# Four-layer graph network on one core: 12 of the last layer's 49 dense row steps moved from the attention projection into the second mean aggregation

## The chip, the cores and the metric

The kernel runs on one core of a Trainium2 chip. The metric is the device time of one execution in microseconds (us), lower is better. The engines are named as in the profile: PE (matrix engine), DVE (vector engine), ACT (scalar engine), POOL (GpSimd, which issues the indirect transfers) and SP (the queue that issues the plain transfers).

## The reference

There are 50,000 nodes with 128 features and 25,000 edges, whose destinations are sorted. Four layers follow each other, each a residual with a layer norm:

```python
x = _layernorm(x + _L0_gnn_ref(x, edge_attr_64, W, b, src, dst))       # gated messages, summed by destination
x = _layernorm(x + _L1_gnn_ref(x, edge_index_t, kernel, attention))    # attention, scores clipped to -2..2
x = _layernorm(x + _L2_gnn_ref(x, edge_index, 0, W1l, b1, W1r, W2l, b2, W2r))
x = _layernorm(x + _L3_gnn_ref(x, edge_index, qw, kw, ln_gamma, ln_beta, out_w, out_b))

def _L2_gnn_ref(...):                    # two mean aggregations
    h = relu(_sage(x, src, dst, W1l, b1, W1r))
    return _sage(h, src, dst, W2l, b2, W2r)
def _sage(x, src, dst, Wl, b, Wr):
    return _mean_aggr(x, src, dst, n) @ Wl.T + b + x @ Wr.T

def _gat_forward(x, ...):                # layer L3
    Q, K = x @ qw, x @ kw                # per head, 4 heads of 32
    alpha = (Q[:, row] * K[:, col]).sum(-1) / scale
    a = exp(alpha - seg_max[col]); a = a / denom[col]
    h = segment_sum(Q[:, row] * a, col)
    h = layernorm(h) * ln_gamma + ln_beta
    return (h * sigmoid(h)) @ out_w + out_b
```

A node without an incoming edge has `h = 0` in the last layer, so its result is `layernorm(x + c)` with one constant row `c`. The kernel computes that for all 50,000 nodes first (the "dense rows") and then overwrites the rows of the nodes that have edges.

## The kernel before, in words

Edge rows lie in 128 partitions of 196 slots. A step handles J = 4 slots of each partition, so a stage over the edges has 49 steps (`STEPS`); one step of the dense rows handles 8 rows of each partition, 1024 nodes, and there are 49 of these as well (`DENSE_STEPS`; the last, the tail, has 848 nodes).

The program is a list of stages, each with its own loop on every engine. The function `pipeline(eng, looped, stages, per)` writes such a loop: a list of (lag, function, count), where in iteration s the function handles step s - lag. The first and last iterations are written out, the others run in a hardware loop of `per` iterations a turn. The order within an iteration is the order of the list, and each engine executes its instructions strictly in that order. Engines wait for each other through semaphores only (`wait_done`: the step is finished; `wait_free`: the buffer's last use two steps ago is finished; `wait_landed`, `wait_drained`: a transfer in or out of the buffer has completed).

The stages that matter here:

- **gat**, the attention of layer L1 (about 545 to 1015 us). DVE adds up each step's scores in `add_others`, `add_scores`, `leaky_scores` and `clip_scores`. Each used a semaphore of its own (`others`, `e0`, `e1`, `e2`).
- **sage2**, the second mean aggregation (about 1914 to 2180 us). In a step POOL gathers 4 times 128 source rows (L803; buffers four steps deep), DVE sums them by destination (L1634, `running_sum`), takes the means (L2080, L2084), PE transposes and multiplies (L961, L1161 to L1169), ACT copies the transposes out (L1277, `sage_copies`), DVE takes the moments of the sum (`x3_moments`, L2133, L1587, lag 2), ACT the square root (L1254, lag 2), DVE inverts it (`x3_shifts`, L1612, L1602, L1598, lag 3), and ACT writes the normed rows (`new_x3`, L1427, lag 3). SP loads two row blocks and stores two for each step. The loop is four iterations a turn.
- **att1**, the attention projection (about 2182 to 2500 us). In a step POOL gathers again, DVE passes node rows back along the runs (L1877, `spread_row`, four a step), PE transposes both and multiplies by the query and key weights (L1192, L1198), ACT copies out (L1277 twice, L1449, L1452), DVE multiplies and sums per head (L2161, L2165, lag 2). All 49 dense steps ran here, one an iteration: SP loads 512 KB (L607), DVE adds the constant row (`nodes_x3_more`, L2172), takes the moments (L1581, L1587, `nodes_x3_moments`), ACT takes the root (L1254, lag 1), DVE inverts and makes the shifts (L2184, L1598, lag 1), ACT writes 8 normed rows a partition (L1268, lag 1) and SP stores 512 KB (L614, lag 2). The loop is two iterations a turn.

The dense steps wrote into rings of two buffers, `node_in` and `node_out`; `own_rows` was a ring of two too.

## Time and profile before

| | us |
|---|---|
| median of 3 runs (lowest to highest) | 2859.24 (2841.92 to 2860.3) |
| time of the profiled execution | 2861.17 |
| span of the profiled execution | 2859.5 |
| DVE busy in it | 2280.2 (80%) |
| PE, ACT, POOL busy | 1851.7, 1735.6, 1698.8 |

The span is what the profile draws. The time of an execution is what the runs measure, here 1.7 us more than its span. An engine's busy share over the whole span says little in this program, because every stage is limited by something else. It is read stage by stage.

### The profile page before, as it was taken

What the parts mean: (1) busy time and instruction counts of PE and PEld (TensorE: products, weight loads), DVE (VectorE), ACT (ScalarE), POOL (GpSimd) and SP (SyncE); (2) the same over time, 40 slices, a digit from 0 to 9 for tenths busy, and PEclk for the clock granted to TensorE, in tenths of its full rate; (3) what the DMA queues carried; (4) which work ended last, traced back from release to release, by engine and by line L of the source; (5) the groups of instructions that cost most, each with busy time, mean ns of one, the idle gap of its engine ahead of it and who ended that gap; (6) DMA issues with size and microseconds to landing.
All of it is one profiled execution on the core that took longest, in us unless ns stands there. A gap on an engine that the chain in (4) does not pass through costs nothing. (4 is left out here: it accounts for less than half of the span.)

```text
span 2859.5 us, 51576 instructions
## 1 busy us (share of the span) xinstructions
PE 1851.7 (65%) x9787; PEld 1368.6 (48%) x9787; DVE 2280.2 (80%) x9061; ACT 1735.6 (61%) x4459; POOL 1698.8 (59%) x1605
## 2 busy tenths in 40 slices
PE   5676766466666626777777666658886666656673
PEld 4565656344544414445455333336665555534442
DVE  7887887899999927887788688857776999888882
ACT  3554545333333316887778688864555888858885
POOL 7777777266656664333333666637776776327775
PEclk8777777789888867998899899989997888767876
DMA  6777877445444437999899788868886888734441
GB/s 202 240 245 230 256 247 236 139 79 85 79 79 84 71 52 256 350 330 325 325 338 344 248 291 291 298 216 252 265 263 211 292 295 294 264 136 160 163 160 52
DMA packets 280133, 625.06 MB, mean 219 GB/s; under 512 B 51230, under 2 KB 84649, under 8 KB 280055
## 3 DMA queue, kind: packets, MB, share of 16 engines
q1 hardware_dynamic: 207543, 523.73, 53.6%
q0 software_dynamic: 72512, 100.52, 16.1%
q14 instruction: 58, 0.48, 0.1%
q8 instruction: 20, 0.33, 0.0%
HBM read 342.76 MB, written 285.23 MB: 220 GB/s over the span
## 5 line engine op out<-in xcount | busy, mean ns | idle before, releaser
L1268 ACT ACTIVATE node_out<-node_in,n_shift,n_root 128x128 f32<-128x128 f32 (+1 forms) x1176 | 468.1, 482 | 85.5 <-DVE n_shift L1598 85.4
L795 POOL DMA_INDIRECT sums<-gat_sums,dst_safe_i x196 | 185.7, 948 | 306.1 <-DVE pre L2027 256.5
L916 POOL DMA_INDIRECT out_dram<-node_x2t,out_index x196 | 208.7, 1065 | 156.7 <-ACT node_x2t L1485 96.3
L803 POOL DMA_INDIRECT src_rows<-x_table,row_i x200 | 201.4, 1007 | 129.9 <-issue 52.2
L803 POOL DMA_INDIRECT sums<-x_table,row_i x192 | 193.8, 1010 | 87.3 <-issue 50.0
L1581 DVE BATCH_NORM_STATS2 n_stats<-node_in 128x6 f32<-128x256 f32 (+1 forms) x588 | 209.4, 419 | 25.4 <-DMA node_in<-y_nodes 14.2
L862 POOL DMA_INDIRECT gat_sums<-src_rows,add_idx x100 | 160.9, 1609 | 112.9 <-issue 24.7
L803 POOL DMA_INDIRECT own_rows<-in_x_dram,dst_safe_i x196 | 191.1, 975 | 59.7 <-issue 58.8
L1277 ACT ACTIVATE t_a<-ps 128x512 f32<-128x512 f32 (+1 forms) x198 | 115.8, 585 | 175.0 <-PE ps L961 167.9
L862 POOL DMA_INDIRECT gat_sums<-sums,add_idx x96 | 153.5, 1599 | 92.9 <-issue 31.7
L961 PE MATMUL ps<-ident,msg 128*128 128x128 f32 x590 | 105.3, 305 | 122.5 <-DVE msg L2111 57.4
L1277 ACT ACTIVATE t_b<-ps 128x512 f32<-128x512 f32 (+1 forms) x198 | 115.9, 586 | 104.7 <-PE ps L961 104.6
L961 PE MATMUL ps<-ident,own_rows 128*128 128x128 f32 x588 | 101.9, 302 | 94.2 <-DMA own_rows<-in_x_dram,dst_safe_i 90.0
L961 PEld LDWEIGHTS ps<-ident,msg 128*128 128x128 f32 x590 | 72.3, 154 | 179.4 <-issue 131.4
L1090 PE MATMUL ps<-node_x2t,w1r_t 128*128 128x512 f32 x196 | 110.1, 689 | 56.2 <-ACT node_x2t L1368 55.6
L1192 PE MATMUL ps<-qw_sb,t_a 128*128 128x128 f32 x392 | 71.9, 340 | 96.1 <-ACT t_a L1277 96.1
L1101 PE MATMUL ps<-w2r_t,node_h1t 128*128 128x128 f32 (+1 forms) x784 | 126.8, 311 | 0.0
L961 PEld LDWEIGHTS ps<-ident,own_rows 128*128 128x128 f32 x588 | 75.5, 154 | 101.7 <-DMA own_rows<-in_x_dram,dst_safe_i 97.2
L1039 PE MATMUL ps<-alpha,node_in 128*128 128x196 f32 x392 | 95.2, 397 | 40.6 <-DVE junk L1917 38.2
L837 POOL DMA_INDIRECT src_rows<-in_x_dram,src_i x100 | 100.3, 1003 | 30.4 <-issue 30.2
L1634 DVE SCALAR_TENSOR_TENSOR acc<-acc,keep,src_rows 128x129 f32<-128x129 f32 x200 | 71.1, 356 | 58.9 <-DMA src_rows<-h_table,row_i 32.8
L1101 PEld LDWEIGHTS ps<-w2r_t,node_h1t 128*128 128x128 f32 (+1 forms) x784 | 106.2, 210 | 22.7 <-issue 22.7
(424 smaller groups left out, 6618.9 us busy)
## 6 DMA issues: line engine op xcount, KB each, us to landing
own_rows<-x_table SPq DMA_DIRECT2D x245, 256.0 KB, 3.3
node_in<-in_x_dram SPq DMA_DIRECT2D x96, 512.0 KB
x_table<-node_out SPq DMA_DIRECT2D x96, 512.0 KB
x_table<-new_rows SPq DMA_DIRECT2D x147, 256.0 KB
gat_sums<-node_x2t SPq DMA_DIRECT2D x49, 528.0 KB, 4.0
acc_dump<-acc SPq DMA_DIRECT2D x98, 264.0 KB
node_sums<-gat_sums SPq DMA_DIRECT2D x48, 528.0 KB
h_table<-node_h SPq DMA_DIRECT2D x48, 512.0 KB, 5.2
```

The lines of the kernel that those rows point to most:

```text
L795: g_.indirect_dma_start(out=to[:, g.b, j, 0:width], out_offset=None, in_=tab, in_offset=bass.IndirectOffsetOnAxis(ap=indices(j), axis=0)). ...
L803: g_.indirect_dma_start(out=to4[g.q][:, j, 0:F], out_offset=None, in_=tab, in_offset=bass.IndirectOffsetOnAxis(ap=indices(j), axis=0)).the ...
L837: g_.indirect_dma_start(out=src4[g.q][:, j, 0:F], out_offset=None, in_=x[:, :], in_offset=bass.IndirectOffsetOnAxis(ap=at_tile(src_i, g, j ...
L862: g_.indirect_dma_start(out=gat_sums[:, :], out_offset=bass.IndirectOffsetOnAxis(ap=add_idx[:, g.q, j:j + 1], axis=0), in_=src4[g.q][:, j, ...
L916: g_.indirect_dma_start(out=out[:, :], out_offset=bass.IndirectOffsetOnAxis(ap=out_index[:, t:t + 1], axis=0), in_=wide_new[:, g.b, j, :], ...
L961: last = te.transpose(ps[bank][g.b][:, j * F:(j + 1) * F], tiles[:, j, 0:F], ident[:, :])
L1039: last = te.matmul(ps[0][j // 2][:, at], past_at[g.b][:, j * P:(j + 1) * P], slot_score[:, :], start=True, stop=True)
L1090: last = te.matmul(ps[1][h][:, :], w1r_t[:, :], node_x2t[:, g.b, h * J * F:(h + 1) * J * F], start=True, stop=True)
L1101: last = te.matmul(ps[3][bank][0:pn, i * F:(i + 1) * F], node_h1t[:, g.b, j * F:j * F + pn], w2r_t[:, :], start=False, stop=i == J - 1)
L1268: last = sc.activation(to[0:pn, g.b, j, :], rows[0:pn, g.b, j, 0:F], ACT.Identity, bias=NORM[k][2][0:pn, g.b, j:j + 1], scale=root[0:pn, j ...
L1277: sc.activation(to[:, g.b, 0:jn * F], ps[bank][g.b][:, 0:jn * F], ACT.Copy).then_inc(L[copied].sem, 1)
L1581: last = v.bn_stats(NORM[k][0][0:pn, g.b, j:j + 2, :].rearrange("p j c -> p (j c)"), rows[0:pn, g.b, j:j + 2, 0:F].rearrange("p j f -> p f ...
```

## The change

Of the 49 dense steps of the last layer, 12 (`SPACED`) are moved into sage2, one in every fourth iteration; the remaining 37 stay in att1, in three of every four iterations (36 and the tail). `spaced(lag, stage)` calls a stage for those steps s whose s mod 4 is 0, `packed(lag, stage)` for those whose s mod 4 is 0, 1 or 2. On SP the spaced loads have a lag of 1 and the stores a lag of 5; on DVE the moments have a lag of 2 and the inverses 3; on ACT the root has 2, the first four of the eight rows 3 and the last four 4. The spaced steps use one buffer, the packed steps three (a third input and a third output buffer come from `node_y`). In att1 the loops of SP, ACT and DVE become four iterations a turn, `own_rows` becomes four buffers deep (`own4`), and SP's loads and stores get other lags. SP now waits for the end of the dense stores of layer L2 before sage2 instead of before att1. In gat the semaphores `others`, `e0` and `e1` become one, `scored`, which counts three a step. No arithmetic is changed.

```diff
+SPACED = 12
+def wait_third_free(eng, signal, g):
+    if isinstance(g, Spaced):
+        eng.wait_ge(signal.sem, g.index() + signal.base)
+    elif isinstance(g.of4, int) and g.of4 == 0:
+        eng.wait_ge(signal.sem, signal.base + SPACED)
+    else:
+        eng.wait_ge(signal.sem, g.index() + (signal.base - 2))
+def spaced(lag, stage):
+    def turn(g):
+        if g.q == 0 and not (isinstance(g.of4, int) and g.of4 >= SPACED):
+            stage(Spaced(g))
+    return (lag, turn, STEPS)
+def packed(lag, stage):
+    def turn(g):
+        if g.q < 3:
+            stage(Packed(g))
+    return (lag, turn, STEPS)
...
-        PER = {"accd": J, "ended": J, "spread": J, "dpe": 2, "dact": 2}
+        PER = {"scored": 3, "accd": J, "ended": J, "spread": J, "dpe": 2, "dact": 2}
...
+            def load_last_nodes(g):
+                D = flow["nodes4"]
+                wait_third_free(sp, D["n_row"], g)
+                for lo, hi in parts(g):
+                    sp.dma_start(in3[g.b][lo:hi, :, :], node_rows(x3_table, SLOTS, g)[lo:hi]).then_inc(rows_in3.sems[g.b], 16)
...
             L = flow["sage2"]
             wait_all(sp, flow["sage1"]["stored"])
+            wait_all(sp, flow["nodes3"]["n_out"])
...
-            pipeline(sp, STEPS, edges((0, both), (1, dump), (4, store)))
+            pipeline(sp, STEPS, edges((0, both), (1, dump), (4, store)) + [spaced(1, load_last_nodes), spaced(5, store_last_nodes)], per=4)
...
-            pipeline(sp, DENSE_FULL, edges((0, load_own_back(L, x3_table, own_rows))) + [nodes(0, load_nodes(D, x3_table, SLOTS, "n_row"))]
-                     + edges((2, store_q)) + [nodes(2, store_nodes(D, out, 0))])
+            pipeline(sp, DENSE_FULL, edges((0, load_own4)) + [packed(1, load_last_nodes)]
+                     + edges((3, store_q)) + [packed(3, store_last_nodes)], per=4)
...
-            pipeline(act, STEPS, edges((3, new_x3), (2, root), (0, sage_copies)), per=4)
+            pipeline(act, STEPS, edges((3, new_x3), (2, root)) + [spaced(2, last_node_root)] + edges((0, sage_copies))
+                     + [spaced(3, last_node_rows(0, J)), spaced(4, last_node_rows(J, DJ))], per=4)
...
-            pipeline(act, DENSE_FULL, [nodes(1, roots(D, "n")), nodes(1, normed_rows(D, "n", node_in, node_out, "n_row", "n_out"))]
-                     + edges((1, queries_keys_out), (0, att_copies)))
+            pipeline(act, DENSE_FULL, [packed(1, last_node_root), packed(1, last_node_rows(0, DJ))]
+                     + edges((1, queries_keys_out), (0, att_copies)), per=4)
...
-            pipeline(dve, STEPS, edges((3, x3_shifts), (0, sources_landed), run[0], run[1], (2, x3_moments), run[2], run[3],
-                                       (0, means)), per=4)
+            pipeline(dve, STEPS, edges((3, x3_shifts), (0, sources_landed), run[0], run[1], (2, x3_moments), run[2], run[3], (0, means))
+                     + [spaced(3, last_inverses), spaced(3, last_shifts), spaced(2, last_more), spaced(2, last_moments)], per=4)
...
-            pipeline(dve, DENSE_FULL, edges(spread[0]) + [nodes(1, node_inverses)] + edges(spread[1]) + [nodes(1, node_shifts)]
-                     + edges(spread[2], (2, products), spread[3], (2, score_sums)) + [nodes(0, nodes_x3_more), nodes(0, nodes_x3_moments)])
+            pipeline(dve, DENSE_FULL, edges(spread[0]) + [packed(1, last_inverses)] + edges(spread[1]) + [packed(1, last_shifts)]
+                     + edges(spread[2], (2, products), spread[3], (2, score_sums)) + [packed(0, last_more), packed(0, last_moments)], per=4)
```

DVE in sage2, the end of one iteration and the start of the next, before (`acc`, `msg` and `edge` are the sums, means and counts; `e_root`, `e_shift` the norm of the edge rows):

```order
L2080 RECIPROCAL edge<-acc 128x4 [waits accd]
L2084 TENSOR_SCALAR msg<-acc,edge 128x128 [waits rcp,tr_a]
L2084 TENSOR_SCALAR msg<-acc,edge 128x128 x3
L1612 RECIPROCAL e_root<-e_root 128x4 [waits e_rt]
L1602 TENSOR_TENSOR e_root<-e_root,canon 128x4 [waits e_rc]
L1598 SCALAR_TENSOR_TENSOR e_shift<-e_stats,e_root 128x4 [waits scaled]
```

The same place after, in an iteration that carries the moments of a dense step (one of four):

```order
L2200 RECIPROCAL edge<-acc 128x4 [waits accd]
L2204 TENSOR_SCALAR msg<-acc,edge 128x128 [waits rcp,tr_a]
L2204 TENSOR_SCALAR msg<-acc,edge 128x128 x3
L2262 TENSOR_TENSOR node_in<-node_in,local_bc 128x1024 [waits n_in0]
L2270 BN_STATS n_stats<-node_in 128x6 [waits n_row,n_pre]
L2270 BN_STATS n_stats<-node_in 128x6 x3
L2274 TENSOR_SCALAR n_root<-n_stats 128x8 [waits n_bn]
L1732 RECIPROCAL e_root<-e_root 128x4 [waits e_rt]
L1722 TENSOR_TENSOR e_root<-e_root,canon 128x4 [waits e_rc]
L1718 SCALAR_TENSOR_TENSOR e_shift<-e_stats,e_root 128x4 [waits scaled]
```

Six dense instructions now stand between the means of one step and the norm of an earlier step.

ACT in sage2 after, in the iteration that carries the dense root (`node_out` rows follow later):

```order
L1545 ACTIVATE new_rows<-ps,e_shift,e_root 128x128 [waits e_nm,stored1]
L1545 ACTIVATE new_rows<-ps,e_shift,e_root 128x128 x3
L1352 ACTIVATE e_root<-e_root 128x4 [waits e_ve]
L1375 ACTIVATE n_root<-n_root 128x8 [waits n_ve]
L1395 ACTIVATE t_a<-ps 128x512 [waits mm,tr_a]
L1395 ACTIVATE t_b<-ps 128x512 [waits mm,tr_b]
```

Before, the copies `t_a` and `t_b` stood right behind the root of `e_root`. Now the dense root, which waits for DVE's dense moments, stands ahead of them.

DVE in att1 before, one iteration (they were all alike):

```order
L1877 SCALAR_TENSOR_TENSOR msg<-msg,undone,own_rows 128x128 [waits spread,tr_b,own1]
L2184 RECIPROCAL n_root<-n_root 128x8 [waits n_rt]
L1877 SCALAR_TENSOR_TENSOR msg<-msg,undone,own_rows 128x128 [waits spread]
L1598 SCALAR_TENSOR_TENSOR n_shift<-n_stats,n_root 128x8 [waits n_rc]
L1877 SCALAR_TENSOR_TENSOR msg<-msg,undone,own_rows 128x128 [waits spread]
L2161 TENSOR_TENSOR pre<-new_rows,gate 128x512 [waits score,cp_c,newd]
L1877 SCALAR_TENSOR_TENSOR msg<-msg,undone,own_rows 128x128 [waits spread]
L2165 TENSOR_REDUCE alpha<-pre 128x16 [waits pre]
L2172 TENSOR_TENSOR node_in<-node_in,local_bc 128x1024 [waits n_in1]
L1581 BN_STATS n_stats<-node_in 128x6 [waits n_nm,n_row,n_pre]
```

The same engine after: the fourth iteration, which has no dense moments (and ends at the TENSOR_REDUCE), and the next one, which has no inverse and no shift:

```order
L2314 TENSOR_REDUCE alpha<-pre 128x16 [waits pre]
L1997 SCALAR_TENSOR_TENSOR msg<-msg,undone,own_rows 128x128 [waits spread,tr_b,own0]
L1997 SCALAR_TENSOR_TENSOR msg<-msg,undone,own_rows 128x128 [waits spread] x2
L2310 TENSOR_TENSOR pre<-new_rows,gate 128x512 [waits score,cp_c,newd]
L1997 SCALAR_TENSOR_TENSOR msg<-msg,undone,own_rows 128x128 [waits spread]
L2314 TENSOR_REDUCE alpha<-pre 128x16 [waits pre]
L2262 TENSOR_TENSOR node_in<-node_in,local_bc 128x1024 [waits n_in0]
```

So in four iterations three dense steps are left on DVE, with their instructions in the order they had.

## Rows read from the trace of the kernel before

**Rows 1.** Busy time by stretch: gat, sage2, att1; PE, PEld, DVE, ACT, POOL, clock, DMA, GB/s

```profile
600.00:1000.00 400.00, 261.42 (x1430) 193.91 (x1431) 372.56 (x2022) 127.41 (x339) 252.09 (x159) 0.89 0.49 81
1942.00:2142.00 200.00, 166.76 (x1064) 125.13 (x1063) 149.42 (x599) 101.47 (x274) 151.53 (x160) 1.00 0.82 260
2200.00:2450.00 250.00, 159.56 (x953) 143.69 (x952) 225.46 (x555) 210.96 (x520) 176.94 (x169) 0.81 0.88 295
```

**Rows 2.** Groups of instructions in sage2 (1942 to 2142): count, busy, mean, idle before

```profile
L803 POOL DMA_INDIRECT sums<-h_table,row_i x80 | 76.4, 955 | 24.4 <-issue 20.7 <-DVE acc L1634 3.7
...
L1634 DVE SCALAR_TENSOR_TENSOR acc<-acc,keep,sums 128x129 f32<-128x129 f32 x80 | 28.5, 356 | 20.3 <-DMA sums<-h_table,row_i 13.1 <-issue 1.3
```

**Rows 3.** Timeline of DVE in sage2, two iterations: start, duration, idle before

```profile
2011.21 0.23 DVE L1612 RECIPROCAL e_root<-e_root 128x4 f32<-128x4 f32 x1
...
2012.26 0.85 DVE L1634 SCALAR_TENSOR_TENSOR acc<-acc,keep,sums 128x129 f32<-128x129 f32 x2 [0.28 <-issue]
...
2015.12 0.88 DVE L2084 TENSOR_SCALAR msg<-acc,edge 128x128 f32<-128x128 f32 x4
2015.91 0.17 DVE L1612 RECIPROCAL e_root<-e_root 128x4 f32<-128x4 f32 x1
...
2017.30 0.86 DVE L1634 SCALAR_TENSOR_TENSOR acc<-acc,keep,sums 128x129 f32<-128x129 f32 x2 [0.73 <-DMA sums<-h_table,row_i]
...
2020.96 0.17 DVE L1612 RECIPROCAL e_root<-e_root 128x4 f32<-128x4 f32 x1
```

**Rows 4.** Timeline of ACT in sage2, one iteration

```profile
2016.90 0.60 ACT L1277 ACTIVATE t_a<-ps 128x512 f32<-128x512 f32 x1 [1.99 <-issue]
...
2017.87 1.51 ACT L1427 ACTIVATE new_rows<-ps,e_shift,e_root 128x128 f32<-128x128 f32 x4
2019.24 0.23 ACT L1254 ACTIVATE e_root<-e_root 128x4 f32<-128x4 f32 x1
```

**Rows 5.** Timeline of DVE in att1, two iterations

```profile
2299.87 0.35 DVE L1877 SCALAR_TENSOR_TENSOR msg<-msg,undone,own_rows 128x128 f32<-128x128 f32 x1 [0.59 <-issue]
...
2302.70 1.22 DVE L2172 TENSOR_TENSOR node_in<-node_in,local_bc 128x1024 f32<-128x1024 f32 x1
...
2305.56 0.42 DVE L1587 TENSOR_SCALAR n_root<-n_stats 128x8 f32<-128x8 f32 x1
2306.00 0.35 DVE L1877 SCALAR_TENSOR_TENSOR msg<-msg,undone,own_rows 128x128 f32<-128x128 f32 x1
...
2306.76 0.16 DVE L1598 SCALAR_TENSOR_TENSOR n_shift<-n_stats,n_root 128x8 f32<-128x8 f32 x1
...
2312.44 0.35 DVE L1877 SCALAR_TENSOR_TENSOR msg<-msg,undone,own_rows 128x128 f32<-128x128 f32 x1 [0.59 <-issue]
```

**Rows 6.** Timeline of ACT in att1, one iteration

```profile
2306.01 0.21 ACT L1254 ACTIVATE n_root<-n_root 128x8 f32<-128x8 f32 x1
2306.96 3.19 ACT L1268 ACTIVATE node_out<-node_in,n_shift,n_root 128x128 f32<-128x128 f32 x8 [0.74 <-DVE n_shift L1598]
2310.05 0.58 ACT L1449 ACTIVATE new_rows<-ps 128x512 f32<-128x512 f32 x1
...
2311.96 0.21 ACT L1254 ACTIVATE n_root<-n_root 128x8 f32<-128x8 f32 x1
```

**Rows 7.** Timeline of PE in att1, in the same iteration

```profile
2305.66 1.91 PE L1192 MATMUL ps<-qw_sb,t_a 128*128 128x128 f32 x8 [2.78 <-ACT t_a L1277]
...
2309.62 0.60 PE L961 MATMUL ps<-ident,msg 128*128 128x128 f32 x4
```

**Rows 8.** Groups of instructions in att1 (2182 to 2500)

```profile
L803 POOL DMA_INDIRECT src_rows<-x_table,row_i x99 | 104.9, 1059 | 41.9 <-issue 28.2 <-PE ps L961 13.7
...
L2172 DVE TENSOR_TENSOR node_in<-node_in,local_bc 128x1024 f32<-128x1024 f32 (+1 forms) x49 | 59.6, 1217 | 1.1 <-DMA node_in<-x_table 1.0
```

**Rows 9.** Timeline of POOL in att1, the gather that overlaps a dense addition of DVE

```profile
2303.03 1.70 POOL L803 DMA_INDIRECT sums<-x_table,row_i  x1 [0.30 <-issue]
2305.04 0.94 POOL L803 DMA_INDIRECT sums<-x_table,row_i  x1 [0.30 <-issue]
```

**Rows 10.** Timeline of DVE in gat, around the second addition of the scores

```profile
802.35 0.16 DVE L1974 TENSOR_TENSOR key<-key 128x4 f32<-128x4 f32 x1
802.47 0.16 DVE L1932 TENSOR_TENSOR edge<-edge 128x4 f32<-128x4 f32 x1
```

124 lines of the change are left out of this document (93 added, 31 removed).

## The prediction

> **What bounds the kernel now.** I read the busy time by stretch first, then the timelines of the two stages that the change touches, because the share of the whole span mixes them.
>
> In sage2 POOL is the pace. It issues 160 gathers in 200 us, 1.25 us each, so a step of four takes 5.0 us [rows 1]. Busy time says 151.5 of 200 only, but 0.30 us stands before each gather in which POOL waits for nothing that another engine could give [rows 2]. DVE waits for gathered rows instead: 13.1 us in this stretch for half of its steps [rows 2]. PE runs at a granted clock of 1.00, the DMA engines are 0.82 busy at 260 GB/s [rows 1].
>
> In att1 DVE is the pace. Two iterations take 12.57 us (2299.87 to 2312.44) [rows 5], 25.1 us for four, and DVE is 90% busy (225.5 of 250 us) [rows 1]; one of the two iterations begins with 0.59 us of "issue", the turn of the loop [rows 5]. ACT is close behind: from root to root 5.95 us (2306.01 to 2311.96), its only idle time 0.74 us, for DVE's shift [rows 6]. POOL needs 1.06 + 0.30 us a gather, 5.4 us a step [rows 8], and so has 0.8 us to spare.
>
> The work moves from a stage where DVE has little slack to one where it had none. The question is whether sage2's slack is large enough.
>
> **sage2: what a dense step costs there.** First the slack. The iteration from 2011.21 to 2015.91 had no wait for rows (0.28 us "issue" only) and took 4.70 us; the next took 5.05 with 0.73 us of waiting, 4.60 without what exceeds the 0.28 [rows 3]. So DVE alone needs 4.65 us a step, 18.6 us for four, and the gathers allow 20.0. Slack: 1.4 us in four steps.
>
> Then the load. From the dense addition to the variance is 2.86 us (2302.70 to 2305.56) and the variance takes about 0.17 more [rows 5] (0.42 in the row shown; I take the shorter, that of other small operations such as the one at 2306.76). Inverse and shift are two small operations, 0.2 and 0.16 us, with a drain between them: 0.45. Together 3.5 us. 18.6 + 3.5 = 22.1 us for four steps, and DVE is the pace.
>
> Then ACT. In the iteration with the dense moments the dense root stands ahead of the copies, and it waits until DVE has done the moments, 3.0 us after the means. That delays PE's product, but DVE's next moments are two iterations off, so it is covered. Further on it is not: ACT's copies of step 4i are through 1.9 us after the means (2016.00 to 2017.87) [rows 3, 4]; then come four dense rows, 1.55 us (half of 3.09, from 2306.96 to 2310.05) [rows 6]; then `new_x3`, 1.37, and the root, 0.23 [rows 4]. That is 5.05 us, and DVE asks for the root after 4.65. DVE waits some 0.4 us once in four steps, or nothing if the stage runs ahead there. I take 22.4 us for four, and 12 x (22.4 - 20.0) = **+29 us**. Bounds: if the 3.5 us shrinks by what small waits absorb, 21.5, +18; the high end comes with the rivals.
>
> What is hidden: ACT's dense work, 3.1 + 0.2 us in four steps on an engine that is busy 101 of 200 us [rows 1]. SP's loads and stores: SP now waits for the rows of the dense step before (one buffer), and behind that wait stand the loads of the own rows of the next step; these are needed more than one iteration later, so 2 us of delay have cover. Four iterations of slack in the gather buffers keep POOL going through DVE's 3 us. The earlier wait of SP for the layer L2 stores costs nothing that I can find: POOL's first gather of sage2 comes after sage1's last scattered row, long after the last dense store was issued.
>
> The lengthened gather: one that overlaps the dense addition took 1.70 us, not 0.94 [rows 9]. In sage2, where POOL is the pace, that would be 0.76 us a dense step, 20.8 us for four. It stays under DVE's 22.4, so it adds nothing. [...]
>
> **att1: what is saved.** DVE loses the 3.5 us of one dense step in four and one of two loop turns (0.6): 25.1 - 4.1 = 21.0 us. That is a floor, not the time. POOL: 16 x 1.36 = 21.8, less the lengthened gather of one addition, 21.4. And the ring through ACT: root, DVE's inverse, second spread and shift, eight rows, query, gate and two copies take 5.95 us [rows 6], three times in four iterations: 17.9. The fourth iteration has no rows; there ACT's copies wait for PE, which multiplies and transposes for 4.56 us (2305.66 to 2310.22) [rows 7] at a clock of 0.81 [rows 1], and then ACT copies again. From copy to copy this is 4.8 us as the row shows it and some 3.6 if PE ran at full clock; I take 4.4, nearer to the row. 17.9 + 4.4 = 22.3 us, and the ring is the pace. 12 x (22.3 - 25.1) = **-34 us**; bounds -44 (POOL's floor, 21.4) and -19 (23.5, if the short iteration delays the next one too). DVE hardly waited for its own rows, so the deeper ring of these gives nothing more. The wait of DVE's products for the gate of two steps ago, new in the short turn, is about 0.5 us and lies inside the 22.3.
>
> **gat: the merged semaphore.** `add_scores` started 0.12 us after the operation before it [rows 10]. It now waits for a register operation that computes three times the step number and stands behind another wait. DVE is 93% busy there [rows 1], so 0.1 us a step shows: 49 x 0.1 = 5 at most, **+4 us**, bounds 0 and 8. Nothing in the trace shows this operation in this place.
>
> **Sum.** -34 + 29 + 4 = -1 us on the profiled execution of 2861 us. The median of the runs is 2859.2, so 2858 us. What 12 dense steps give back in att1 they take in sage2, because DVE's slack there is 1.4 us in four steps and a dense step needs 3.5.
>
> **Rivals.**
>
> *A, sage2 is cheap and att1 gives all it can.* DVE's small waits overlap with the dense operations (21.5 us for four, +18), att1 reaches POOL's floor (-44), gat costs nothing: -26, **2833 us**. For it: the idle gaps of 0.1 to 0.3 us on DVE may be filled. Against: they are drains between dependent operations and stay.
>
> *B, POOL stays the pace in sage2.* The move costs the lengthened gathers only: 20.8 us for four, +9; with -34 and +4 this is -21, **2838 us**. [...] For it: POOL is the pace today. Against: DVE's 22.1 us, which nothing hides.
>
> *C, slower: sage2's transfers.* Four steps move 4 x 1288 KB (gathered 256, own 2 x 256, dumped 264, stored 256), 5.3 MB, which fits the 260 GB/s of the stage. A dense step adds 1024 KB: 6.3 MB. At 260 GB/s that takes 24.3 us, +52 in all; with -34 and +4 this is +22, **2881 us**, and with att1 at its weak end +37. It decides from 22.4 us for four steps on, which is 282 GB/s. The place where it would show is the gathered rows landing late although POOL is ahead. For it: the DMA engines are 0.82 busy and would be 0.97 by proportion at an unchanged 20 us. Against: 295 GB/s at 0.88 in att1 [rows 1], where dense transfers take part.
>
> *D, the short iteration in att1 disturbs its neighbours.* Three long iterations after a short one do not settle at 5.95; 23.5 us for four, -19: in all +14, **2873 us**.
>
> *E, it does not do what it says*: the moved steps leave att1 at POOL's pace. That is the floor of 21.4 us in A, and it limits no more than the ring does.
>
> **How the numbers follow.** My forecast has 0.48, A 0.15, B 0.10, C 0.15, D 0.12. A measurement of this kernel tells about 1% (29 us) from no change. The likeliest case has 2858, with its own bounds 2843 to 2870. The range 2834 to 2882 takes in B, D, most of A and half of C, and leaves out less than 2 in 10. Faster by over 1% (below 2831) needs A and more: 0.16. Slower by over 1% (above 2888) needs C with D: 0.17. Within 1%: 0.67.
>
> **What would show it.** In sage2, DVE's waits for gathered rows almost vanish and POOL's waits for DVE's sums grow; four steps take 22.4 us, and the stage grows by some 29 us. PE's clock may fall below 1.00. Gathers that overlap the dense addition take 1.7 us. In att1 four steps take about 22.3 us, with one short iteration, and ACT's wait for the shift is 0.7 us throughout. In gat a step grows by about 0.1 us. I am wrong if sage2 keeps 20 to 21 us for four steps, or if att1 shrinks by less than 20 us.

## Result and the profile after

The changed kernel takes 2861.59 us (median of 16 runs, 2848.62 to 2872.06), the kernel before 2849.52 us in the runs beside it (16 runs). The ratio is 1.0042, with a 95% interval of 1.0025 to 1.0059: 12 us slower, where -1 was forecast. A second comparison, in another session, gives 1.0021 (1.0004 to 1.0037), 6 us. The profiled execution takes 2862.23 us, 1 us more than the profiled one of before (2861.17 us), which is longer than all 16 runs of that kernel (highest 2860.3). So the two traces alone hide what the medians show, and a good part of the study is about that.

Busy time by stretch of the kernel after, with the columns of [rows 1] (the att1 stretch is 210 us long here, since the stage starts later):

```profile
600.00:1000.00 400.00, 273.65 (x1424) 203.16 (x1423) 371.07 (x2014) 125.56 (x334) 249.52 (x156) 0.84 0.48 79
1942.00:2142.00 200.00, 158.04 (x962) 117.11 (x960) 161.62 (x604) 120.24 (x330) 149.40 (x150) 0.97 0.86 285
2240.00:2450.00 210.00, 140.65 (x899) 127.95 (x898) 177.91 (x447) 166.68 (x398) 164.90 (x148) 0.85 0.84 280
```

In sage2 POOL issued 150 gathers in 200 us instead of 160, and DVE is busy 12 us longer. The granted clock is 0.97 instead of 1.00. The groups of the same stretch (compare [rows 2]):

```profile
L900 POOL DMA_INDIRECT sums<-h_table,row_i x77 | 75.0, 974 | 27.5 <-issue 21.0 <-DVE acc L1754 6.5
...
L1754 DVE SCALAR_TENSOR_TENSOR acc<-acc,keep,sums 128x129 f32<-128x129 f32 x72 | 25.6, 355 | 10.3 <-issue 1.5 <-DMA sums<-h_table,row_i 1.4 <-DMA acc_dump<-acc 1.2
```

DVE's 13.1 us of waiting for gathered rows are down to 1.4, and POOL waits 6.5 us for DVE in this group where it waited 3.7: the pace has passed to DVE, though POOL's buffers hide most of that within this stretch. POOL's gathers are also longer here, 974 ns on average instead of 955. The timeline of DVE in sage2 has the dense operations in one iteration and the wait for ACT's root three iterations later:

```profile
2044.44 1.21 DVE L2262 TENSOR_TENSOR node_in<-node_in,local_bc 128x1024 f32<-128x1024 f32 x1
2045.77 1.42 DVE L2270 BATCH_NORM_STATS2 n_stats<-node_in 128x6 f32<-128x256 f32 x4
...
2062.28 0.18 DVE L1732 RECIPROCAL e_root<-e_root 128x4 f32<-128x4 f32 x1 [0.32 <-ACT e_root L1352]
...
2066.87 1.20 DVE L2262 TENSOR_TENSOR node_in<-node_in,local_bc 128x1024 f32<-128x1024 f32 x1
```

From addition to addition, four steps, it is 22.43 us (2044.44 to 2066.87). At the end of the stage POOL, which had been up to four steps ahead, stands still until DVE has caught up and the last sums are dumped:

```profile
2172.79 0.95 POOL L900 DMA_INDIRECT src_rows<-h_table,row_i  x1 [0.30 <-issue]
...
2192.49 0.95 POOL L912 DMA_INDIRECT fix_acc<-acc_dump,fix_idx  x1 [16.26 <-DMA acc_dump<-acc]
```

In the trace of before that wait is 4.47 us. I read it as no cost of its own: it is where the 22.4 us a turn, hidden from POOL by its buffers, are paid.

In att1 POOL never waits in the middle of the stage (compare [rows 9]), and PE waits for rows that have not landed. POOL, then PE:

```profile
2340.55 1.40 POOL L900 DMA_INDIRECT sums<-x_table,row_i  x1 [0.30 <-issue]
2342.26 1.68 POOL L900 DMA_INDIRECT src_rows<-x_table,row_i  x1 [0.30 <-issue]
2344.24 0.95 POOL L900 DMA_INDIRECT src_rows<-x_table,row_i  x1 [0.30 <-issue]
```

```profile
2336.65 1.12 PE L1059 MATMUL ps<-ident,src_rows 128*128 128x128 f32 x4 [3.19 <-DMA src_rows<-x_table,row_i]
```

### The profile page after: what moved, and what is told of

The parts are those of the page before. It is cut to its first block and busy times, and to the rows that moved or that the text cites. A ratio compares the mean times of both kernels' runs of the same rounds, so it can differ in the third digit from the quotient of the medians.

```text
span 2860.5 us, 51307 instructions
## 1 busy us (share of the span) xinstructions
PE 1875.3 (66%) x9787; PEld 1384.6 (48%) x9787; DVE 2272.9 (79%) x9061; ACT 1734.1 (61%) x4459; POOL 1711.8 (60%) x1605
## 5 line engine op out<-in xcount | busy, mean ns | idle before, releaser
L1366 ACT ACTIVATE node_out<-node_in,n_shift,n_root 128x128 f32<-128x128 f32 (+1 forms) x784 | 311.9, 483 | 34.1 <-DVE n_shift L1718 33.9
L900 POOL DMA_INDIRECT src_rows<-x_table,row_i x200 | 209.2, 1046 | 116.0 <-issue 53.6
L1701 DVE BATCH_NORM_STATS2 n_stats<-node_in 128x6 f32<-128x256 f32 x392 | 139.5, 418 | 15.2 <-DMA node_in<-y_nodes 13.1
L1385 ACT ACTIVATE node_out<-node_in,n_shift,n_root 128x128 f32<-128x128 f32 (+1 forms) x296 | 119.0, 483 | 20.0 <-DVE n_shift L2284 20.0
L900 POOL DMA_INDIRECT src_rows<-h_table,row_i x100 | 100.7, 1007 | 33.7 <-issue 28.0
```

Of the source, the lines that this page charges most:

```text
L900: g_.indirect_dma_start(out=to4[g.q][:, j, 0:F], out_offset=None, in_=tab, in_offset=bass.IndirectOffsetOnAxis(ap=indices(j), axis=0)).the ...
L1366: last = sc.activation(to[0:pn, g.b, j, :], rows[0:pn, g.b, j, 0:F], ACT.Identity, bias=NORM[k][2][0:pn, g.b, j:j + 1], scale=root[0:pn, j ...
L1385: last = sc.activation(out3[g.b][0:pn, j, :], in3[g.b][0:pn, j, :], ACT.Identity, bias=shift3[g.b][0:pn, j:j + 1], scale=root3[g.b][0:pn, ...
L1701: last = v.bn_stats(NORM[k][0][0:pn, g.b, j:j + 2, :].rearrange("p j c -> p (j c)"), rows[0:pn, g.b, j:j + 2, 0:F].rearrange("p j f -> p f ...
```

## The experiments

All stage lengths below are read the same way: from the first gather of a stage to the first gather (after att1: the first scatter) of the next, in the one profiled execution of each kernel. The edited kernels are compared with the kernel before in the same session. x2, which no edit touches, shows the spread of one execution. Eight of the kernels leave out work or bytes to test a cause: e2, e4, e8, e10, e11, e15, e5 and e16.

| kernel | ratio to before (95%) | x2 | sage2 | att1 |
|---|---|---|---|---|
| before | 1 | 517.6 | 267.2 | 368.0 |
| after | 1.0042 (1.0025 to 1.0059) | 524.2 | 296.0 | 340.3 |
| after_again | 1.0021 (1.0004 to 1.0037) | 513.9 | 297.7 | 344.1 |
| e1_scored | 0.9997 (0.9977 to 1.0017) | 513.9 | 267.0 | 366.9 |
| e2_no_spaced | 0.9889 (0.9866 to 0.9912) | 515.3 | 266.8 | 347.1 |
| e3_turns4 | 1.0005 (0.9988 to 1.0021) | 524.0 | 266.0 | 365.0 |
| e4_thin | 0.9975 (0.9957 to 0.9993) | 513.4 | 282.4 | 340.0 |
| e8_thin_lag2 | 1.0045 (1.0028 to 1.0062) | 508.0 | 310.7 | 344.7 |
| e11_thin_rows3 | 0.9959 (0.9942 to 0.9976) | 528.3 | 281.2 | 340.7 |
| e10_slim | 0.9999 (0.9985 to 1.0012) | 516.0 | 293.6 | 341.9 |
| e15_thin_slim | 0.9903 (0.9880 to 0.9925) | 512.7 | 268.3 | 346.2 |
| e5_three | 1.0020 (1.0001 to 1.0040) | 517.9 | 296.0 | 342.0 |
| e9_warm | 0.9996 (0.9981 to 1.0011) | 518.0 | 296.6 | 338.0 |
| e16_three_warm | 0.9969 (0.9951 to 0.9987) | 521.7 | 298.3 | 329.4 |
| e12_stt | 1.0023 (1.0002 to 1.0043) | 520.9 | 298.3 | 341.2 |
| e17_pieces | 1.0044 (1.0024 to 1.0064) | 512.4 | 298.4 | 346.6 |
| e14_all | 1.0033 (1.0013 to 1.0052) | 512.2 | 306.2 | 338.0 |
| e18_quarters_warm | 1.0031 (1.0010 to 1.0051) | 526.4 | 296.6 | 346.0 |
| e19_halves_warm | 1.0024 (1.0003 to 1.0046) | 511.8 | 299.7 | 342.1 |

### The parts of the change alone

**e1_scored.** The kernel before with gat's merged semaphore.

```diff
...
-                wait_done(dve, L["others"], g)
+                wait_part(dve, L["scored"], g, 1)
...
```

> The kernel before with the merged semaphore in gat alone. The term of the forecast was +4 us (0 to 8): a step 0.1 us longer because add_scores waits for a register operation. The changed kernel's trace has the gat stage at 499.8 us against 499.6, which speaks for 0. Theory 'merged semaphore costs nothing': ratio to before 1.000, gat 499 to 501 us. Rival 'it is part of the 12 us that the changed kernel is slower by': ratio 1.0015 or more, gat 503 us or more.

Measured 0.9997. gat took 503.7 us in this profile (the rival asked for 503 or more), 499.6 before and 499.8 after; e3_turns4, which has the old semaphores, took 502.8. All 17 profiles with the merged semaphore have 499.8 to 504.6 us, mean 502.4. So no cost shows, but the stage's length and the ratio (its interval is -7 to +5 us) cannot tell 0 from +4 either. The timeline of DVE can. Here `add_scores` (L1932) and `clip_scores` (L1942) with the operation before each, in e1_scored:

```profile
799.08 0.16 DVE L1974 TENSOR_TENSOR key<-key 128x4 f32<-128x4 f32 x1
799.31 0.16 DVE L1932 TENSOR_TENSOR edge<-edge 128x4 f32<-128x4 f32 x1
...
800.46 0.15 DVE L1979 TENSOR_TENSOR add_idx<-key,dummy_rows 128x4 int32<-128x4 f32 x1
800.57 0.17 DVE L1942 TENSOR_SCALAR edge<-edge 128x4 f32<-128x4 f32 x1
```

The wait that was forecast is there: throughout the hardware loop `add_scores` starts 0.22 to 0.23 us after the operation before it, where it was 0.12 [rows 10]. But `clip_scores` starts 0.10 to 0.12 us after its predecessor instead of 0.18 to 0.19. From the operation before `add_scores` to `clip_scores` the median is 1.42 us, and 1.37 in the kernel before: 0.05 us a step, 2.5 us for 49 steps (an estimate), of which DVE's wait for ACT behind it may hide a part.

**e2_no_spaced.** The 12 dense steps of sage2 are left out, att1 is as in the changed kernel.

```diff
-SPACED = 12
+SPACED = 0
...
-            pipeline(sp, STEPS, edges((0, both), (1, dump), (4, store)) + [spaced(1, load_last_nodes), spaced(5, store_last_nodes)], per=4)
+            pipeline(sp, STEPS, edges((0, both), (1, dump), (4, store)), per=4)
...
```

> The changed kernel without the 12 dense steps in sage2 (their rows of the output are left out altogether); att1 with its 37 steps as in the changed kernel. Theory 'sage2 pays for the dense steps with DVE time, 29 us': sage2 returns to about 267 us, att1 stays at 340, and the time is 28 to 30 us below the changed kernel's, about 2832 us, ratio to before 0.990 to 0.994. Rival 'part of the loss comes from the new shape of the rings and SP's earlier wait, not from the steps': sage2 stays above 272 us and the time falls by less than 24 us.

sage2 is back at 266.8 us, so the other edits in it (SP's earlier wait, the rings) are free, and the 29 us belong to the 12 steps. But att1 took 347.1 us, not 340. That led to the second rhythm, below. The ratio (0.9889, 32 us below the kernel before) is lower than the 0.990 to 0.994 expected, and more than the 21 us by which sage2 and att1 together are shorter here.

**e3_turns4.** The kernel before with loops of four iterations a turn in att1.

```diff
-                     + edges((1, queries_keys_out), (0, att_copies)))
+                     + edges((1, queries_keys_out), (0, att_copies)), per=4)
...
```

(the same in SP's and DVE's loops)

> The kernel before with one edit: the loops of SP, ACT and DVE in att1 have four iterations a turn instead of two. All 49 dense steps stay in att1. Theory 'DVE paces att1, and a turn of its loop costs 0.59 us': four steps fall from 25.1 to 24.5 us, 12 x 0.59 = 7 us less, ratio 0.9975. Rival 'the turn only fills a wait on ACT's ring': unchanged. Second rival, slower: the longer unrolled code costs fetches, four steps above 25.1 us.

No gain that can be measured (1.0005); the stage is 2 to 3 us shorter, not 7. DVE's idle time at the turn fell, but its waits for transfers rose. Waits of DVE between 2200 and 2450 us, the kernel before and then this one (total us, times, longest):

```profile
DVE msg L1877 <- issue: 8.2, 18, 0.6
...
DVE msg L1877 <- DMA own_rows<-x_table: 1.9, 3, 0.8
DVE node_in L2172 <- DMA node_in<-x_table: 0.6, 2, 0.4
```

```profile
DVE msg L1877 <- issue: 5.6, 15, 0.7
...
DVE msg L1877 <- DMA own_rows<-x_table: 2.8, 7, 0.7
DVE node_in L2172 <- DMA node_in<-x_table: 2.1, 4, 0.9
```

Of the 2.6 us that the turns give back, 2.4 return as waits for rows that land later.

### sage2: DVE's work, or the transfers

**e4_thin.** All transfers of the spaced steps stay, their work on DVE and ACT shrinks (ACT writes two of eight rows).

```diff
...
+                n = 1 if isinstance(g, Spaced) else DJ
+                v.tensor_tensor(in3[g.b][0:pn, 0:n, :], in3[g.b][0:pn, 0:n, :],
...
-                for j in range(0, DJ, 2):
+                for j in range(0, 2 if isinstance(g, Spaced) else DJ, 2):
```

> The changed kernel, whose 12 dense steps in sage2 make all their transfers (512 KB in, 512 KB out) but compute thinly: DVE adds the constant to one row of eight and takes one pair's moments of four, ACT writes two rows of eight; the other rows of these steps go out unchanged or stale. DVE's work for a dense step falls from 3.5 to about 1.3 us, below the slack of 1.4 us in four steps. Theory 'DVE's sum of work paces sage2': four steps fall from 22.5 to 20.0 to 20.4 us, the stage by 24 to 29 us. Rival C of the forecast, transfers (6.3 MB in four steps): four steps stay at 22 us or above, and gathered rows land late although POOL is ahead.

Between the two theories: 282.4 us, half of the 29 us gone. What is left is DVE's wait for the dump of an earlier step's sums, which SP begins behind the dense load. Waits between 1942 and 2142 us:

```profile
DVE acc L1754 <- DMA acc_dump<-acc: 12.7, 9, 2.6
```

SP stood at the dense load, for the buffer, 14.3 us in nine times. Two ways to take that wait away, both with the thin work:

**e8_thin_lag2** begins the load one iteration later.

(the part of the line that changes)

```diff
-[spaced(1, load_last_nodes), spaced(5, store_last_nodes)]
+[spaced(2, load_last_nodes), spaced(5, store_last_nodes)]
```

> The thin kernel (12 spaced steps with all their transfers, DVE and ACT do a part of their work, those rows are not finished) with one more edit: SP begins the spaced load one iteration later, lag 2, so that it finds its buffer free. With lag 1 SP stood at that load for 14.3 us in nine times, and DVE waited 12.7 us for the dumps that are queued behind it; sage2 took 282 us, not 267. Theory 'SP's wait ahead of the dumps costs the remaining 15 us': SP's wait for the rows vanishes, sage2 takes 267 to 272 us. Rival 'the bytes of the dense transfers cost it': the dumps still land late, sage2 stays at 278 us or above.

The longest sage2 of all, 310.7 us. Waits of DVE:

```profile
DVE node_in L2263 <- DMA node_in<-x_table: 32.9, 9, 5.6
```

One lag more is too late for the rows themselves: DVE waits up to 5.6 us for them. Of the two lags the change's 1 is the better one, at least with the thin work.

**e11_thin_rows3** lets ACT finish the rows one iteration earlier instead.

(the part of the line that changes)

```diff
-[spaced(3, last_node_rows(0, J)), spaced(4, last_node_rows(J, DJ))]
+[spaced(3, last_node_rows(0, J)), spaced(3, last_node_rows(J, DJ))]
```

> The thin kernel again (spaced load at lag 1, all transfers, a part of the work on DVE and ACT, those rows not finished), with one edit: ACT writes its second part of the rows at lag 3 too, one iteration earlier, so that SP finds the buffer free at lag 1. The try to avoid SP's wait with a later load came out slower: DVE then waited 32.9 us for the rows themselves. Theory 'SP's wait in front of the dumps costs the 15 us that are left in the thin kernel': SP's wait for the dense rows falls from 14.3 us to under 4, DVE's for the dumps from 12.7 to under 4, sage2 from 282 to 267 to 273 us. Rival 'the bytes cost it': sage2 stays above 278 us.

SP's wait for the dense rows is gone from the list altogether, and the stage is still 281.2 us:

```profile
DVE acc L1754 <- DMA acc_dump<-acc: 8.9, 8, 2.6
```

My theory of SP's wait falls. The dumps are late although SP no longer stands at the dense load ahead of them.

**e10_slim** keeps the work and moves an eighth of the bytes, and **e15_thin_slim** does both reductions.

```diff
+                    n = 1 if isinstance(g, Spaced) else DJ
+                    sp.dma_start(in3[g.b][lo:hi, 0:n, :], node_rows(x3_table, SLOTS, g)[lo:hi, 0:n])
```

(and the same for the store)

> The changed kernel, whose 12 spaced steps do all their work on DVE and ACT but move an eighth of their bytes (64 KB in, 64 KB out instead of 512 each; seven of eight rows of these steps are not the right ones). Theory 'DVE's sum of work paces sage2': four steps stay at 22.4 us, the stage shrinks by less than 5 us from 296. Rival 'transfers': the stage falls below 280 us, the kernel by 16 us or more.

> Both reductions together in the 12 spaced steps of sage2: the thin work of DVE and ACT, and an eighth of the bytes (64 KB in, 64 KB out); their rows are not the right ones. Thin work alone left 14 of the 29 us (sage2 281 to 282), also where SP found its buffer free; fewer bytes alone took 2 to 4 us off. Theory 'two limits stand close to each other: DVE's work (22.4 us for four steps) and, below it, the burst of 1 MB of dense load and store in one iteration, which makes the dump of the sums land late': with both away sage2 is 267 to 270 us. Rival 'the spaced steps cost something that is neither work nor bytes (waits, order, the longer iteration)': sage2 stays at 276 us or above.

Busy time between 1942 and 2142 us, e10_slim, then e15_thin_slim:

```profile
1942.00:2142.00 200.00, 157.22 (x956) 116.59 (x957) 162.54 (x610) 119.06 (x328) 150.81 (x152) 0.97 0.77 244
```

```profile
1942.00:2142.00 200.00, 170.78 (x1061) 126.06 (x1060) 161.46 (x648) 110.26 (x305) 151.44 (x160) 0.98 0.85 268
```

With 244 GB/s instead of 285 POOL still issues 152 gathers, not 160; four steps of DVE stay at 22.42 us, and the stage gives back 2.4 us. So the work is what paces the changed kernel, and the transfers are not (rival C). That it is DVE's work and not ACT's, which e4_thin reduces too, no run separates; the trace says it: in the changed kernel DVE waits for ACT 3.4 us in eight times in this stretch, 0.4 us of the 2.4 that a turn of four steps has grown by. With work and bytes both away the stage is 268.3 us and has its 160 gathers, and four steps take 20.05 us. There are two limits, one behind the other: DVE at 22.4 us for four steps, and at about 21.3 (e4_thin's mean) the bytes of load and store. Taking only DVE's work away gives back half.

### att1: why 24 us and not 34

In the eight profiles whose att1 is that of the changed kernel (after, after_again, e2, e4, e8, e10, e11, e15) the stage takes 340.0 to 347.1 us, mean 343.1, against 367.5 for before and e1: -24.4. I counted DVE's turns of four steps in each trace, from dense addition to dense addition, without the first, in which the stage fills. Most take 22.0 to 23.1 us, but some take 23.78 to 23.84, several in a row. The stage's length follows their number: none gives 340.3 and 340.0 us, one 341.9 and 340.7, three 344.1 and 344.7, five 346.2, seven 347.1. In that rhythm the short iteration falls on a granted clock of PE of 0.50. Timeline of PE in e2_no_spaced, then in the kernel after, both around a short iteration:

```profile
2292.74 2.07 PE L1292 MATMUL ps<-qw_sb,t_a 128*128 128x128 f32 x8 [2.78 <-ACT t_a L1397]
2294.60 1.91 PE L1298 MATMUL ps<-kw_sb,t_b 128*128 128x128 f32 x8
2296.30 1.06 PE L1061 MATMUL ps<-ident,src_rows 128*128 128x128 f32 x4
2297.16 1.06 PE L1061 MATMUL ps<-ident,msg 128*128 128x128 f32 x4
```

```profile
2350.88 1.15 PE L1290 MATMUL ps<-qw_sb,t_a 128*128 128x128 f32 x8 [2.78 <-ACT t_a L1395]
2351.87 1.06 PE L1296 MATMUL ps<-kw_sb,t_b 128*128 128x128 f32 x8
2352.76 0.60 PE L1059 MATMUL ps<-ident,src_rows 128*128 128x128 f32 x4
2353.20 0.60 PE L1059 MATMUL ps<-ident,msg 128*128 128x128 f32 x4
```

The same four groups take 5.5 us in the one (2292.74 to 2298.22) and 2.9 in the other (2350.88 to 2353.80), and in the short iteration ACT waits for them. The granted clock is 0.50 in the one and 1.00 in the other (from 2292.70 to 2298.30 us and from 2350.80 to 2353.90): eight products take 1.91 to 2.07 us at 0.50 and 1.06 to 1.15 at 1.00. Both times PE had stood idle for 2.78 us just before.

One short iteration at the lower clock is not enough. The kernel after has four of them (0.50 to 0.54 over the first microsecond of the products), and each but the last is followed by one or two at 1.00: the turn that ends with one takes 22.2 to 22.6 us, the next, where there is one, 22.94 or 22.95, and the stage is 340.3 us all the same. Over these eight traces and that of e5_three (below) every one of the 24 turns of 23.78 to 23.84 us has its eight products at 1.6 us or more in the short iteration before it and in its own, and a granted clock of 0.50 over the first microsecond of these products. Of the 75 others 73 have at most one of the two, and all but two of these take 21.5 to 23.2 us.

**after_again.** The changed kernel once more.

> The changed kernel once more, for a second profile and a better median. The two first profiles differ by 1 us, the medians by 12. Theory 'the short iteration of att1 runs in one of two rhythms, set by PE's granted clock in it': this profile, or others of this code, shows stretches of 23.8 us for four steps in att1 (the kernel without the spaced steps had nine such in a row) next to 22.8, and att1 takes 340 to 352 us. Rival 'the 12 us lie outside the two stages': att1 is 340 us again and a stage that the change does not touch (x2 was 524 us, against 514 to 518) is longer than in the kernel before.

It has three turns of 23.8 us and 344.1 us in att1, and its x2 is shorter than in the kernel before. The first theory holds, the rival (x2) does not, in this profile.

**e9_warm.** Filler on PE, in three of four iterations.

```diff
             def queries_keys(g):
+                wait_free(pe, L["newd"], g)
+                if g.q:
+                    for j in range(2 * J):
+                        c = slice(j % J * F, (j % J + 1) * F)
+                        te.matmul(ps[2][g.b][:, c], ident[:, :], qw_sb[:, :, :].rearrange("f h d -> f (h d)"), start=True, stop=True)
                 wait_done(pe, L["cp_a"], g)
-                wait_free(pe, L["newd"], g)
```

> The changed kernel with filler on PE in att1: eight extra products of 128x128 in three of four iterations, while PE waits for ACT's copies; what they write is overwritten by the real products. Theory 'PE's clock sets the rhythm of the short iteration': the granted clock in att1 rises from 0.85 to above 0.95, four steps fall from 22.8 to 22.3 us or less and never show 23.8, the time falls by 5 to 12 us. Rival 'POOL is the pace of att1 (16 gathers at 1.11 + 0.30 us are 22.6)': the clock rises, four steps stay at 22.6 to 22.9 us. Slower: the filler delays PE's products, four steps above 23 us.

Busy time and PE's waits between 2240 and 2450 us:

```profile
2240.00:2450.00 210.00, 168.28 (x1336) 157.35 (x1336) 178.13 (x447) 166.70 (x395) 164.62 (x149) 0.96 0.84 278
```

```profile
PE ps L1059 <- DMA src_rows<-x_table,row_i: 19.6, 9, 4.0
```

The clock rises to 0.96, the runs of 23.8 us are gone, att1 takes 338.0 us and the kernel is 0.25% below after_again (0.9996 against 1.0021 in one session). It is level with the kernel before. But four steps still take 22.0 to 22.6 us, and two single turns 23.7 and 23.8. In those the short iteration is at a granted clock of 1.00 (1.16 us for the eight products), and PE waits 3.8 and 4.0 us for gathered rows: POOL is the next limit.

**e5_three.** Three gathers a step instead of four.

```diff
...
-                for j in range(J):
+                for j in range(3 if L is flow["att1"] else J):
```

> The changed kernel with three gathers a step in att1 instead of four (the fourth row block keeps old data, so the scores of a quarter of the edges are not the right ones). POOL's work falls by a quarter, PE, ACT and DVE do what they did. Theory 'POOL is the pace of att1: 16 gathers at 0.95 + 0.30 us and three lengthened ones, 22.4 to 22.8 us in four steps': without it the ring through ACT is left, four steps take 22.3 us or less, PE no longer waits for gathered rows. Rival 'the ring and its two rhythms (22.8 and 23.8) are the pace': four steps stay at 22.6 to 23.8 us, the stage at 340 to 344.

PE's waits for rows vanish, and nothing is won: 342.0 us, four turns of 23.8, clock 0.81. The rival holds, and the theory that POOL alone is the pace falls: the ring through ACT, with PE at 0.50 in the short iterations of these four turns, is as slow as POOL.

**e16_three_warm.** Both edits together.

> att1 with both reductions: three gathers a step instead of four (a quarter of the scores is not the right one) and PE's filler. Three gathers alone left 342 us with stretches of 23.8 us, the filler alone 338 us with PE waiting 14 to 27 us for gathered rows. Theory 'the ring through ACT at PE's lower clock (22.8 to 23.8) and POOL (22.6) are two limits at the same height': with both away the ring is left at PE's full clock, 3 x 5.95 + 3.6 = 21.5 us for four steps (21.2 to 21.9), att1 at 328 to 333 us. Rival 'DVE's in-order turn is the limit': four steps stay at 22.3 us or more, att1 at 336 or more.

```profile
2240.00:2450.00 210.00, 169.57 (x1377) 154.82 (x1375) 180.90 (x456) 171.00 (x410) 119.50 (x118) 1.00 0.83 279
```

Four steps take 22.01 to 22.02 us, nine turns in a row, and att1 329.4 us. The edit that e5_three lacks is the filler, so the 23.8 us turns go with PE's clock. Two limits of nearly one height, as expected; the ring itself needs 22.0 us at a granted clock of 1.00, 0.5 more than I had worked out (21.5).

### What holds the gathers up

**e12_stt.** The dense addition in another form.

```diff
-                v.tensor_tensor(in3[g.b][0:pn, :, :], in3[g.b][0:pn, :, :],
-                                local3_bc[0:pn, None, :].to_broadcast([pn, DJ, F]), ALU.add)
+                v.scalar_tensor_tensor(in3[g.b][0:pn, :, :], in3[g.b][0:pn, :, :], 1.0,
+                                       local3_bc[0:pn, None, :].to_broadcast([pn, DJ, F]), ALU.mult, ALU.add)
```

> The changed kernel with another form of the dense addition in both stages: (rows x 1.0) + constant as one SCALAR_TENSOR_TENSOR instead of a TENSOR_TENSOR, with the same sizes and result. Theory 'the TENSOR_TENSOR form holds up POOL's gathers (0.95 becomes 1.70 us, 31 us in all in att1), the other form does not, as its small instances in sage2 do not (0.957 us)': the mean gather in att1 falls from 1.11 to about 0.96 us, and if POOL is the pace there four steps fall from 22.8 to 22.3 us, the stage by 4 to 8 us. Rival 'any long instruction of DVE with two inputs in its memory does it': mean gather stays at 1.10, no gain. Slower: the form runs at a lower rate, above 1.22 us for 128x1024.

**e17_pieces.** The addition as four pieces.

```diff
+                for j in range(0, DJ, 2):
+                    made = v.tensor_tensor(in3[g.b][0:pn, j:j + 2, :], in3[g.b][0:pn, j:j + 2, :],
+                                           local3_bc[0:pn, None, :].to_broadcast([pn, 2, F]), ALU.add)
...
```

> The changed kernel with the dense addition as four TENSOR_TENSORs of 128x256 instead of one of 128x1024, in both stages. The scalar_tensor_tensor form had left the mean gather in att1 at 1.11 us, so the form is not the cause. Theory 'a long instruction with two inputs holds POOL's gather up until it ends': with pieces of 0.35 us a gather is held for 0.35 us at most, no gather of 1.7 us is left, the mean falls from 1.11 to 1.00 us or less. Rival 'what counts is the sum of such work': mean 1.09 to 1.12. The time: DVE's work grows by 0.1 to 0.3 us a dense step, so no gain, ratio to before 1.002 to 1.006.

One group of gathers in att1, of the kernel after, of e12_stt and of e17_pieces (compare [rows 8]):

```profile
L900 POOL DMA_INDIRECT src_rows<-x_table,row_i x100 | 113.8, 1138 | 31.7 <-issue 29.6 <-DMA x_table<-new_rows,fix_idx 1.5 <-PE ps L1059 0.6
```

```profile
L900 POOL DMA_INDIRECT src_rows<-x_table,row_i x100 | 113.4, 1134 | 31.7 <-issue 30.2 <-DMA x_table<-new_rows,fix_idx 1.5
```

```profile
L900 POOL DMA_INDIRECT src_rows<-x_table,row_i x100 | 101.6, 1016 | 38.0 <-issue 30.8 <-PE ps L1059 5.7 <-DMA x_table<-new_rows,fix_idx 1.5
```

The form is not the cause; the hold follows the length of one instruction. Summed over the 196 gathers of att1, the time above 0.95 us each is 31 us in the kernel after (37 additions, 0.85 each), 32 in e12_stt and 10 in e17_pieces. In the kernel before it was 22 us for 49 additions, 0.45 each: POOL waited for PE there, 13.7 us in the group of [rows 8] and 13.2 in the other one, and an addition that falls on an idle POOL can leave the gathers as they are: that of 2296.24 us, 1.22 us long, lies within 1.77 us in which POOL waits for PE, and the gather behind it takes 0.95 us. The four pieces leave the sum of this work as it was or above, and only the single instruction is shorter (0.42 us); why it holds a gather back, no run shows. The pieces did not make the kernel faster: att1 346.6 us. DVE's addition takes 1.42 us instead of 1.22, three times in four steps.

### Attempts at a version that beats both

**e14_all** joins e9_warm's filler, e12_stt's form and another order of ACT in sage2.

```diff
-            pipeline(act, STEPS, edges((3, new_x3), (2, root)) + [spaced(2, last_node_root)] + edges((0, sage_copies))
-                     + [spaced(3, last_node_rows(0, J)), spaced(4, last_node_rows(J, DJ))], per=4)
+            pipeline(act, STEPS, edges((3, new_x3), (2, root)) + [spaced(5, last_node_rows(J, DJ))] + edges((0, sage_copies))
+                     + [spaced(2, last_node_root), spaced(3, last_node_rows(0, J))], per=4)
```

> The changed kernel with three edits together: PE's filler in att1, the SCALAR_TENSOR_TENSOR form of the dense addition in both stages, and in sage2 ACT's order changed (the dense root behind the copies, the second four dense rows an iteration later, ahead of the copies). The stages separate them. sage2: if DVE's wait for ACT's root (3.4 us in eight times) is ACT's order, it goes, and the stage falls from 296 to 291 us. att1: 338 us with the filler alone, 332 to 335 if the addition's form frees POOL as well. In all 10 to 14 us below the changed kernel, ratio to before 0.997 to 1.000. Rival: the shift of ACT's rows delays SP's load and with it the dumps, sage2 above 296 us.

The rival came true: sage2 306.2 us. DVE's waits for the root fell only from 3.4 to 2.4 us, SP's wait for the dense rows rose from 24.5 to 35.9, and this appeared:

```profile
DVE acc L1758 <- DMA acc_dump<-acc: 9.9, 8, 2.3
```

**e18_quarters_warm** and **e19_halves_warm** join the filler with pieces in att1 alone (`n = 2` and `n = 4` in the loop of e17_pieces, one piece for the spaced steps).

> The changed kernel with PE's filler in att1 and, in att1 alone, the dense addition as four pieces of 128x256 (1.42 us together instead of 1.22); sage2 keeps one piece, since DVE is its pace. All results as in the reference. Theory 'att1 has two limits of one height, PE's clock in the ring and the gathers held up by the long addition': with both eased, and no work left out, four steps fall from 22.8 to 22.2 us, the stage from 340 to 344 us to 330 to 334, ratio to before 0.996 to 0.999, 8 to 12 us below the changed kernel. Rival 'the 0.2 us more on DVE a dense step lengthen the ring by as much, three times in four steps': four steps 22.6 us or more, the stage 336 us or more.

> As the kernel before it, with two pieces of 128x512 instead of four of 128x256: less on DVE (1.3 us together), a gather held for 0.7 us at most. By the same theory 330 to 336 us for att1; the rival says that the halves still hold gathers long enough for POOL to stay at 22 us or more, and the stage stays at 336 to 338 us.

The theories fell: 346.0 us, as e18's rival said, and 342.1 us, longer than the 336 to 338 of e19's. In e18 POOL needs only 20.3 to 21.1 us for 16 gathers where it does not wait, PE's clock is 1.00, and four steps take 22.6 to 24.5 us all the same. Waits between 2240 and 2450 us, of DVE and then of ACT:

```profile
DVE node_in L2268 <- DMA node_in<-x_table: 7.2, 9, 1.3
```

```profile
ACT n_root L1379 <- DVE n_root L2281: 12.5, 14, 1.4
```

DVE waits for the dense rows (in e9_warm 3.6 us) and its longer addition makes ACT wait for the variance. With POOL and PE eased, DVE and the dense load set the pace, no lower than the limits before; that is read from the waits, and no run takes these two away. No version that does all the work beat the kernel before; e9_warm is level with it.

## Why the prediction was wrong, point by point

**sage2 (+29 us): right.** Four steps take 22.43 us (22.4 forecast), the stage +28.8 us in the first profile and +30 on average over seven profiles with that code. e2 shows that it is the steps, e10 that it is not their bytes. DVE's slack of 1.4 us, the 3.5 us of a dense step and ACT's 0.3 to 0.4 us are all in the trace. What the forecast did not see is the second limit close below: "ACT's dense work", SP's wait and the bytes were costed at nothing behind DVE, and that is right only as long as DVE is slower. e4 and e11 put that limit at 14 to 15 us of the 29.

**gat (+4): too high.** The wait that the forecast put down to a register operation is there, 0.1 us a step (0.22 to 0.23 us in e1, 0.12 before), but the forecast left out what follows: about half of it comes back where `clip_scores` starts earlier. What is left is 0.05 us a step, 2.5 us at most, and no stage length or median shows it.

**att1 (-34): the step that failed.** It is -27.7 us in the first profile and -24 on average. The mechanism is the forecast's, a ring through ACT with POOL close behind; both were sized too short. Two steps of it were mis-sized. First, "POOL: 16 x 1.36 = 21.8, less the lengthened gather of one addition, 21.4". The 1.06 us was a mean over a stage in which POOL often waited, so that many additions fell on no gather. With POOL busy throughout it is 16 x (0.95 + 0.30) = 20.0 and 3 x 0.85 for the additions, 22.6 us, which is what POOL does. I had the row that shows it, 1.70 against 0.94 us [rows 9], and used the mean [rows 8]. Second, the ring: "From copy to copy this is 4.8 us as the row shows it and some 3.6 if PE ran at full clock; I take 4.4". The short iteration has no single value: its four groups on PE took 5.5 us at a granted clock of 0.50 (e2) and 2.9 at 1.00 (the kernel after). Where it is at 0.50 in every turn, four steps take 23.8 us, and 22.7 on average elsewhere, close to what POOL needs. e16 shows 22.0 with both limits away, below the forecast's 22.3.

**Rivals.** A and B needed a cheap sage2, which DVE's work excludes. The short waits that A would have filled stayed: from 1942 to 2142 us DVE's second operation of the norm (L1722) waits for the first 2.9 us in 18 times, 3.3 in 20 before. C (transfers in sage2) falls with e10. D came nearest in its sum, 23.5 us for four steps and +14 us in all; its mechanism, a short iteration that disturbs its neighbours, is what the 23.8 us turns are, with PE's clock as the cause (e9, e16).

**The sum.** +30 in sage2 and -24 in att1 are +6 us, and gat adds 0 to 2.5. The two comparisons gave +12 (7 to 17) and +6 (1 to 11). So the stages explain the second fully and the first in large part; whether the rest is more than the sessions' spread stays open. Single profiles leave gaps of that size elsewhere too: in e2 the two stages are 21 us shorter than before and the medians 32 (25 to 38). The forecast's -1 lies nearer to the measured sum than its terms do, because +4 for gat made up for a part of the 10 us that att1 was short; that part is luck. No stage that the change leaves alone is longer throughout: x2 is 508 to 528 us in the table, in kernels with the same code for it.

## What to carry to other kernels

Moving work from a stage with no slack to one with little gives back what exceeds the slack, and the stage that is relieved gains only down to its next limit. Here POOL, the ring with PE at 0.50 in the short iteration, and DVE with the dense load all stand between 22 and 24 us for four steps, so easing one of them brought 7 us of 2860 at best (e9_warm against after_again); the test that tells is to take two away at once. A mean over a stage in which an engine often waits is no price for that engine when it will be busy throughout: price the events (so many holds of 0.85 us), not the mean.

## What the runs showed of the hardware that I had not expected

The loop of att1 settled into one of two rhythms, the slower one where its short iteration fell on a granted clock of PE of 0.50 (not 1.00) turn after turn. Four steps of one code took 22.7 us on average or 23.83, the latter in runs of up to seven turns, and the stage was up to 7 us longer for it. A single short iteration at the lower clock cost nothing (22.2 to 22.6 us in the kernel after); the 23.83 came only where it was so in one turn after the other. With eight filler products in three of four iterations (e9_warm, clock 0.96 from 2240 to 2450 us) the runs were gone, and with POOL relieved as well (e16_three_warm, clock 1.00) every settled turn took 22.0 us.

DVE's dense addition, one instruction of 1.22 us, holds back the gathers that a busy POOL issues meanwhile: one takes 1.68 us (2342.26) instead of 0.95, and 0.85 us for each addition on average over att1 (31 us for 37; 32 us in the other form, e12_stt). As four instructions of 0.42 us (e17_pieces) it holds them back by a third of that, 10 us.
